# A retention block with an FP4 feed-forward on one core: z formed with tokens in rows, gate and up in three banks, set-up cut into five parts, a new order on every engine

## What is computed

```
Q = xpos(xn W_Q); K = xpos(xn W_K, downscale); V = xn W_V          # 8 heads of 32
scores = (Q K^T) * D,  D[n, m] = gamma_h^(n - m) for n >= m, else 0
Y = scores V;  Yn = (Y - mean) / sqrt(var + 1e-5) per head, times gn_weight, plus gn_bias
gate = silu(xn W_G);  retention = (gate * Yn) W_O
fp4(x): per block of 16 along the row, scale = max|x| / 6, x / scale rounded to the E2M1 grid, times scale
ffn = fp4(silu(fp4(xn) fp4(w_gate)^T) * (fp4(xn) fp4(w_up)^T)) fp4(w_down)^T       # inner width 704
```

## Time and profile before

| | us |
|---|---|
| median of 3 runs | 949.18 (949.08 to 950.0) |
| the profiled execution | 948.74 |
| its span | 946.9 |
| PE busy | 888.8 |
| DVE busy | 895.9 |
| ACT busy | 528.5 |
| POOL busy | 443.7 |

### The profile page before, as it was taken

The page is one execution under the profiler, slowest core; times in us unless marked ns, Lnnn a source line. Parts: engine busy times, 40 slices in busy tenths (PEclk is TensorE's granted clock), DMA queues, the critical chain, the costliest instruction groups (busy, mean ns, idle before and its releaser), DMA issues.

```text
span 946.9 us, 21085 instructions
## 1 busy us (share of the span) xinstructions
PE 888.8 (94%) x8258; PEld 798.1 (84%) x8258; DVE 895.9 (95%) x2220; ACT 528.5 (56%) x1331; POOL 443.7 (47%) x343
## 2 busy tenths in 40 slices
PE   0169999999999999999999999999999999999997
PEld 0158988898989899889988998998899889989986
DVE  5899999999999999999999999999999999999995
ACT  1345565556556655665555566556655655565553
POOL 3564544553454445444544444554445344444543
PEclk9999999999999999999999999999999999999999
DMA  9000000000000000000000000000000000000000
GB/s 281 40 1 12 24 12 24 23 24 13 24 23 19 18 24 24 12 24 24 24 12 24 24 19 17 23 24 12 24 23 24 14 24 23 18 19 24 12 7 17
DMA packets 28259, 24.95 MB, mean 26 GB/s; under 512 B 9088, under 2 KB 27648, under 8 KB 27904
## 3 DMA queue, kind: packets, MB, share of 16 engines
q1 hardware_dynamic: 20224, 18.95, 6.5%
q10 hardware_dynamic: 7936, 4.66, 1.7%
HBM read 15.21 MB, written 8.39 MB: 25 GB/s over the span
## 4 chain that ended last, share of the span: by engine, by line
PE 91%; DVE 5%; POOL 2%; ACT 1%; DMA 0%; issue 0%; SPq 0%; DVEq 0%; POOLq 0%
PE quad L775 11%; PE quad L773 11%; PE quad L774 11%; PE quad L844 4%; PE quad L908 4%; PE bank L850 3%; PE bank L855 3%; PE quad L901 3%; PE bank L774 3%; PE bank L775 3%; PE bank L773 3%; PE bank L830 3%; PE bank L862 3%; PE quad L869 3%; PE quad L878 2%; PE quad L877 2%
## 5 line engine op out<-in xcount | busy, mean ns | idle before, releaser
L392 POOL TENSOR_TENSOR h_quot<-h,h_inv 128x704 f32<-128x704 f32 x64 | 88.9, 1389 | 266.2 <-DVE h_inv L607 266.2
L388 POOL TENSOR_TENSOR rstd<-var_eps,power 128x9 f32<-128x9 f32 x67 | 158.0, 2358 | 38.6 <-DVE var_eps L557 38.5
L774 PE MATMUL quad<-w_gu_lo,xT_hi 128*128 128x352 f32 x512 | 165.1, 322 | 0.0
L775 PE MATMUL quad<-w_gu_hi,xT_lo 128*128 128x352 f32 x512 | 165.1, 322 | 0.0
L773 PE MATMUL quad<-w_gu_hi,xT_hi 128*128 128x352 f32 x512 | 165.0, 322 | 0.0
L376 POOL TENSOR_TENSOR zT_lo<-zT,zT_hi 128x256 fp32r<-128x256 f32 x64 | 51.8, 809 | 164.6 <-ACT zT_hi L677 164.6
L775 PEld LDWEIGHTS quad<-w_gu_hi,xT_lo 128*128 128x128 f32 x512 | 96.2, 188 | 0.0
L773 PEld LDWEIGHTS quad<-w_gu_hi,xT_hi 128*128 128x128 f32 x512 | 96.2, 188 | 0.0
L774 PEld LDWEIGHTS quad<-w_gu_lo,xT_hi 128*128 128x128 f32 x512 | 96.1, 188 | 0.0
L384 POOL TENSOR_TENSOR qk<-qk_cos,qk_sin 128x512 f32<-128x512 f32 x64 | 82.9, 1295 | 7.1 <-DVE qk_sin L531 6.5
L689 ACT ACTIVATE silu<-quad 128x352 f32<-128x352 f32 x64 | 29.8, 465 | 92.2 <-PE quad L775 92.2
(11 more groups left out here) (147 smaller groups left out, 2849.5 us busy)
## 6 DMA issues: line engine op xcount, KB each, us to landing
x_in<-in_L_attn_X_dram SPq DMA_DIRECT2D x64, 128.0 KB, 2.1
out_dram<-y_out SPq DMA_DIRECT2D x64, 128.0 KB, 1.7
sin<-const_sin_dram ACTq DMA_DIRECT2D x1, 2048.0 KB, 11.1
cos<-const_cos_dram ACTq DMA_DIRECT2D x1, 1024.0 KB, 6.4
raw<-in_L_ffn_w_down_dram SPq DMA_DIRECT2D x2, 352.0 KB, 4.0
raw<-in_L_ffn_w_gate_dram SPq DMA_DIRECT2D x1, 512.0 KB, 3.9
raw<-in_L_ffn_w_up_dram SPq DMA_DIRECT2D x1, 384.0 KB, 5.4
w_qkvg<-in_L_attn_W_Q_dram ACTq DMA_DIRECT2D x2, 128.0 KB, 5.0
```

The costliest lines, as they stand in the source:

```text
L388: pool.tensor_tensor(rstd[:], var_eps[:], power[:], ALU.pow).then_inc(rstd_ready, 1)
L392: pool.tensor_tensor(blocks(h_quot[:]), blocks(h[:]), spread(h_inv[:]), ALU.mult).then_inc(h_divided, 1)
L774: pe.matmul(out, hi[:, k], w_lo[:, k], start=False, stop=False)
L775: return pe.matmul(out, lo[:, k], w_hi[:, k], start=False, stop=stop)
```

## The change

The arithmetic of the result stays; what moves is where and when it is done.

1. **z with tokens in rows.** POOL multiplies the gate by weight and by bias, both broadcast over the partitions (`gate_gn`, 128x512), and by `rstd` (`y_gain`). DVE multiplies the transposed-back y by it (`y_part`, in place of `y_hat`), POOL adds the bias part (`z`). PE transposes z (two transposes in place of four), ACT copies the high part out of PSUM and DVE subtracts for the low part (in place of `zT` there and `zT_lo` on POOL). The two ACT instructions with weight and bias go.
2. **Gate and up in three banks.** The 1408 columns are reordered as 384 (the last 192 of gate and of up), 512 and 512. PE issues 6 matmuls of 384 and 12 of 512 columns for 24 of 352. Two of the three groups of tile i + 1 are done at the end of step i.
3. **Small work leaves DVE.** `x_shift`, `x_scale`, `h_scale` and `var_eps` go to POOL, the doubled 64 columns of `hq` to ACT. The reciprocal is taken of the maximum itself, and a factor of nearly 6 follows.
4. **Set-up.** The parts are cut as 768, 1024, 1024, 704 and 704 columns, each handled inside a step of the prologue or of step 0 and 1 (the parts 3 and 4, `w_down`). Three of five divisions move from POOL to DVE. The low part of a transposed weight comes from PE, which adds minus the high part to the transpose in PSUM, and ACT copies it. Loads are reissued in another order, x is loaded 7 tiles ahead by two semaphores, and only the first chunk of the tables is loaded early.
5. **Order.** All engines have a new order inside the step; the down projection of a tile moves wholly to the step two later.

The diff, cut to its core:

```diff
 G = 2
 HG = H // G
 F = 704
-FH = F // 2
+GW = 256
 CHUNKS = S // P
 TILES = B * CHUNKS
...
         b_xT = bank[0]
-        b_qk = b_qkT = bank[1]
-        b_gate = [bank[2], bank[4]]
-        b_up = [bank[3], bank[5]]
-        b_hT = [bank[1], bank[2]]
+        b_qk = bank[1]
+        b_qkT = bank[1]
+        b_gu = [bank[2], bank[3], bank[4][:, 0:2 * F - 4 * GW]]
+        b_vg = bank[5]
         b_kv = bank[3]
-        b_out = bank[4][:, 0:D]
-        b_vg = bank[6]
-        b_yT = [bank[5][:, 0:P], bank[6][:, 0:P]]
-        b_y = b_zT = bank[7]
-
-
+        b_yT = [bank[4][:, 0:P], bank[5][:, 0:P]]
+        b_y = bank[7][:, 0:D]
+        b_zT = bank[7][:, D:2 * D]
+        b_hT = [bank[0], bank[1]]
+        b_out = bank[6][:, 0:D]
+
+
...
+            sp.dma_start(raw_gu[:, 2, :], w_up[F - P:F, :]).then_inc(w_landed[0], 16)
+            sp.dma_start(raw_gu[:, 3:5, :], tiles_of(w_gate, 0, GW)).then_inc(w_landed[1], 16)
...
+                if exists(i + 2):
+                    t = i + 2
+                    pool.wait_ge(rstd_ready, t + 1)
+                    pool.tensor_scalar(x_shift[:], moments[:, 0:1], rstd[:, 0:1], -1.0, ALU.mult, ALU.mult).then_inc(x_shifted, 1)
+                if exists(i - 1):
+                    t = i - 1
+                    pool.wait_ge(rstd_ready, t + 4)
+                    pool.tensor_tensor(heads(y_gain[:]), heads(gate_gn[:, t % 2, 0, :]), spread(rstd[:, 1:], HD), ALU.mult).then_inc(gain_ready, 1)
+                if exists(i):
+                    t = i
+                    pool.wait_ge(rope_cos, t + 1)
+                    pool.tensor_tensor(qk[:], qk_cos[:], qk_sin[:], ALU.add).then_inc(rope_add, 1)
+                    if i == 0:
+                        size(3)
+                        divide(3)
+                    if i == 1:
+                        size(4)
+                        divide(4)
+                        out_low_parts()
+                if exists(i - 1):
+                    t = i - 1
+                    pool.wait_ge(y_scaled, t + 1)
+                    pool.tensor_tensor(z[:], y_part[:], gate_gn[:, t % 2, 1, :], ALU.add).then_inc(z_ready, 1)
+                if exists(i):
+                    t = i
+                    if t == 0:
+                        pool.wait_ge(gn_landed, 32)
+                    pool.wait_ge(gate_silu, t + 1)
+                    pool.tensor_tensor(gate_gn[:, t % 2, :, :], gate[:].unsqueeze(1).broadcast_to([P, 2, D]), gn[:], ALU.mult).then_inc(gate_scaled, 1)
+                    pool.wait_ge(h_inverted, t + 1)
+                    pool.tensor_tensor(blocks(h_quot[:]), blocks(h[:]), spread(h_inv[:]), ALU.mult).then_inc(h_divided, 1)
+                if exists(i + 2):
...
+                if exists(i + 2):
+                    t = i + 2
+                    pool.tensor_scalar(x_scale[:], x_max[:], 1.0 / 6.0, 1e-12, ALU.mult, ALU.max).then_inc(x_scaled, 1)
+                    if i == -2:
+                        qkvg_low_parts(0)
+                if exists(i) or exists(i + 3):
...
+                    if exists(t + 3):
+                        pool.wait_ge(x_moments, t + 4)
+                    pool.tensor_scalar(var_eps[:], moments[:, 1:], EPS, None, ALU.add).then_inc(var_ready, 1)
                     pool.wait_ge(var_ready, t + 4)
...
+            def largest(n):
+                cols, at = bounds(n)
+                dve.wait_ge(w_landed[n], 16 * PART_LOADS[n])
+                dve.tensor_reduce(w_max[:, at], blocks(raw[:, cols]), AX_X, ALU.max,
+                                  apply_absolute_value=True).then_inc(w_scaled[n], 1)
+
+            def invert(n):
+                cols, at = bounds(n)
+                dve.wait_ge(w_scaled[n], 1)
+                dve.reciprocal(w_rec[:, at], w_max[:, at]).then_inc(w_scaled[n], 1)
+                dve.wait_ge(w_scaled[n], 2)
+                dve.tensor_scalar(w_inv[:, at], w_rec[:, at], SIX, 1e12, ALU.mult, ALU.min).then_inc(w_scaled[n], 1)
+
+            def divide(n):
+                cols, at = bounds(n)
+                dve.wait_ge(w_scaled[n], 3)
+                dve.tensor_tensor(blocks(raw[:, cols]), blocks(raw[:, cols]), spread(w_inv[:, at]), ALU.mult).then_inc(w_divided, 1)
+
...
+                    dve.wait_ge(gain_ready, t + 1)
+                    dve.tensor_tensor(y_part[:], b_y[:, 0:D], y_gain[:], ALU.mult).then_inc(y_scaled, 1)
...
+                    if i == -3:
+                        largest(0)
+                        invert(0)
+                        divide(0)
...
+                    if i == -2:
+                        largest(1)
+                        invert(1)
+                        divide(1)
...
+                        dve.wait_ge(mask_landed, 16)
+                    dve.tensor_tensor(probs[:, 0:2, :], quad[:, 0:2, 0:G * P], mask, ALU.mult).then_inc(masked0, 1)
+                    if i == 0:
+                        round_off(3)
+                    if i == 1:
+                        round_off(4)
...
+                    if i == -1:
+                        largest(2)
+                        invert(2)
+                        divide(2)
+                        round_off(1)
+                        centre_values()
...
                     t = i - 1
+                    dve.wait_ge(z_high, t + 1)
+                    dve.tensor_tensor(zT_lo[:], tiles(b_zT), zT_hi[:].bitcast(F32), ALU.subtract).then_inc(z_low, 1)
...
+                    act.wait_ge(h_quant, t + 1)
+                    act.activation(hq[:, F:], hq[:, F - FL:F], ACT.Copy).then_inc(h_twice, 1)
...
+            def high_part(*groups):
+                for m in groups:
+                    hi, lo, shaped = weight_group(m)
+                    act.wait_ge(w_turned, m + 1)
+                    act.activation(hi, shaped(bank[HIGH_BANK[m]]), ACT.Copy).then_inc(w_high, 1)
+
+            def low_part(*groups):
+                for m in groups:
+                    hi, lo, shaped = weight_group(m)
+                    act.wait_ge(w_rest, m + 1)
+                    act.activation(lo, shaped(bank[LOW_BANK[m]]), ACT.Copy).then_inc(w_low, 1)
...
+                act.dma_start(cos[:, 1:, :], cos_d[:, 1:, :]).then_inc(tables_landed[1], 16)
+                act.dma_start(sin[:, 1:, :], sin_d[:, 1:, :]).then_inc(tables_landed[1], 16)
...
+                        turn(4, 5)
+                        turn_rest(4, 5)
+                    if t == 0:
+                        pe.wait_ge(w_low, 6)
+                    if t >= 1:
+                        pe.wait_ge(kv_add, kept_upto(t - 1))
+                    for k in range(KD):
+                        ins = product(b_gu[1], xT_hi[:, KD:], xT_lo[:, KD:], w_gu_hi[:, :, GU_COLS[2]], w_gu_lo[:, :, GU_COLS[2]],
+                                      k, start=k == 0, stop=k == KD - 1)
+                    ins.then_inc(gu_b_ready, 1)
...
+                    for k in range(KD):
+                        ins = pe.transpose(b_zT[:, k * P:(k + 1) * P], z[:, k * P:(k + 1) * P], ident[:])
...
+                    if i == -1:
+                        turn(0, 1)
+                        turn_rest(0, 1)
...
+            def turn_rest(*groups):
+
+                for m in groups:
+                    n, k = divmod(m, 2)
+                    hi, lo, shaped = weight_group(m)
+                    pe.wait_ge(w_high, m + 1)
+                    if 2 <= m <= 4:
+                        pe.wait_ge(w_low, (m - 1, m)[m == 4])
+                    b = bank[LOW_BANK[m]]
+                    for j, src in enumerate(sources(m)):
+                        pe.matmul(b[:, j * P:(j + 1) * P], src, ident[:], start=j == 0, stop=False, is_transpose=True)
+                    pe.matmul(shaped(b), ident_neg[:], hi, start=False, stop=True).then_inc(w_rest, 1)
...
+GU_COLS = [slice(0, 2 * (F - 2 * GW)), slice(2 * (F - 2 * GW), 2 * (F - GW)), slice(2 * (F - GW), 2 * F)]
+GU_PARTS = len(GU_COLS)
+PARTS = ([slice(c.start // P * D, c.stop // P * D) for c in GU_COLS]
          + [slice(NW * D + r * F, NW * D + (r + 1) * F) for r in range(KD)])
-PART_LOADS = [1, 4, 1, 1, 1]
-PART_GROUPS = [2] * len(PARTS)
+PART_LOADS = [4, 2, 2, 1, 1]
+HIGH_BANK = [6, 7, 6, 7, 6, 7, 6, 6, 6, 6]
+LOW_BANK = [1, 5, 1, 5, 5, 3, 6, 6, 6, 6]
```

1001 lines of the change are left out of this document (504 added, 497 removed).

## The result

| | before | after |
|---|---|---|
| median | 949.59 us (949.08 to 950.36, 4 runs) | 933.46 us (932.18 to 934.08, 4 runs) |
| the profiled execution, its span | 948.74, 946.9 | 933.82, 931.9 |

A forecast was written before the change was run, and what follows sets the result against it. PE was taken to pace the kernel, DVE 0.4 us a step behind; 948.7 less 15.9 (steady steps), 13.5 (set-up) and 3 (end) gave 916.3 us, predicted as 916; forecast 906 to 925, range 898 to 936.

The forecast's parts named there:

- The view of what bounds the kernel: Steady part: PE sets the pace at 13.70 us a step, with DVE 0.4 us behind it.
- The steady step: PE's step falls by 0.26 to 13.44 us, 15.9 us over 61 steps; DVE 12.4 us busy, POOL 9.2.
- DVE's stall in `x_diff`: Steady step on DVE: `x_diff`, slow beside POOL's addition for qk, drops from 799 to about 422 ns, saving 0.38 us.
- The rule on the shared port: DVE instructions with two SBUF inputs contend with POOL's SBUF reads; forecast trusted it for streaming work, not for `rstd`'s power.
- The rival in which the port makes the kernel slower: POOL's new streaming collides with DVE: steps up to 15.5 us, 1042 us in all; chance 0.07, shared with another ring.
- The set-up: Work ahead of tile 2: PE starts tile 2 near 70 us instead of 83.4, gaining 13.5 us (4 to 18).
- DVE's entry at 36: Before step 0: 26 us of DVE work, 5 of data waiting, about 2 for the first `xn`, 3 of collisions.
- The 15 and 17.5 us of steps 0 and 1: Lengths of steps 0 and 1: DVE's own work, some 10 and 12 us, plus parts 3 and 4 with collisions.
- DVE's own 4.3 plus 1 of collision each: Steps 0 and 1: DVE's work on parts 3 and 4 adds 4.3 us plus 1 of collision to each.
- the set-up gains nothing: Rival: set-up parts meet collisions and PE's serial turns in steps 0 and 1, 930 us; chance 0.22 shared with DVE bound.
- DVE takes over: Rival: DVE holds the step at 13.70, only set-up and end pay, 932 us; chance 0.22 shared with set-up without gain.
- The end: From tile 63's qk to the finish: about 24.5 us against 27.8, 3 us gained, between 0 and 6.

The follow-up runs named there:

- the three runs on the step: Changed kernel transposing z twice: 945.72 us; changed kernel with one more 256-column DVE instruction per step: 932.10; kernel before without gate's two transposes: 937.60.
- e6: Changed kernel with both loads moved, POOL's z, PE's turns and ACT's magnitude reordered, plus idle transposes in waits of steps 0 and 1: 927.26 us; without those transposes 927.08.

## Why the prediction was right in sign and half as large

**The view of what bounds the kernel: right.** PE paced before and paces after, shown by the three runs on the step.

**The steady step: right, somewhat small.** 13.44 was forecast, 13.43 is measured over the same 61 steps. That agrees by two errors which cancel: a step from tile 3 on is 13.393, and step 2, counted among the 61, is 2.2 us longer than the others (15.59). The 384-column interval was 0.17 us as interpolated. DVE's stall in `x_diff` went as said. DVE is busy 12.7 us a step (378.07 / 400 x 13.43), forecast 12.4, and POOL 9.26, forecast 9.2. There the single terms were off and made up for each other: `x_shift` took 669 and `h_scale` 387 ns, where 200 stood, and `rstd` fell from 2358 to 1835. Behind `x_shift` and `rstd` stand waits for DVE, told below.

**The rule on the shared port: against it for the power, with it for streaming work.** In the steady part `hq` takes 885 ns (880 before), though it starts beside the power, and the new streaming work of POOL cost DVE nothing that PE would feel. In the set-up the collision is real, and as long as the rule of the Trainium skill has it ("SBUF — State Buffer", section "Who interferes with whom"): POOL's low part of qkvg runs as two instructions, from 37.74 to 39.01 and from 38.97 to 40.44 us, and `x_diff` (37.99, 1.29 us) and `x_grid` (39.32, 1.40 us) each end about 0.3 us behind one of them, where 0.43 is their mean; the 5.41 us of the earlier trace rows ended 1.1 behind POOL's 4.73, and takes 1.22 alone. It also works the other way, which the prediction did not ask. In the kernel before, the power starts inside `h_grid` (512.64, 0.88 us) in every steady step and takes 2.38 us; in the changed kernel it starts ahead of it and takes 1.83:

```profile
512.80 2.38 POOL L388 TENSOR_TENSOR rstd<-var_eps,power 128x9 f32<-128x9 f32 x1 [0.45 <-DVE var_eps L557]
```

```profile
515.20 1.83 POOL L457 TENSOR_TENSOR rstd<-var_eps,power 128x9 f32<-128x9 f32 x1
```

```profile
515.51 0.89 DVE L678 SCALAR_TENSOR_TENSOR h_grid<-h_magic,h_diff 128x704 f16<-128x704 bf16 x1
```

The one power of the changed kernel that takes longer (2.41 us at 62.34) starts inside `hq`. In each of these cases 0.71 or 0.72 us of DVE's instruction are left when the power starts, so the 0.5 us that `rstd` fell by read as a wait for DVE. No run varies this by itself. The rival in which the port makes the kernel slower did not come.

**The set-up: this step failed.** "36 + 15 + 17.5 = 68.5, and PE starts tile 2 about 1.5 later, at 70." It was 85.58. With step 2, tile 3 came 17.7 us after the time that the forecast implies (70 + 13.44), which is the whole miss: 17.7, less 2.8 for the steady steps (60 x 0.047), plus 2.7 for the end, is 17.6, and the span is 17.4 us longer than forecast (931.9 against 914.5). Up to tile 2 the 15.6 us are 8.6 at DVE's entry, 7.8 in step 0 and 2.9 in step 1, less 3.7, since PE starts tile 2 2.2 us ahead of DVE's `qk_sin` of it (85.58, 87.75; 83.42, 85.61 before), not 1.5 behind: an error of the sum that worked in its favour. Its terms:
- DVE's entry at 36 was 44.63. The sum took 5 us of waiting for data, before the first tile. It didn't follow SP's queue, in which the load of tile 2 moved behind 0.5 MB of V and G, nor ask what ACT's tables do to it. That wait is 5.92 us, and moving the loads brings the entry to 39.3: shown, 5 to 6 us. DVE's work was right: 29.6 us busy up to there, where 29 stood (26 and 3 of collisions). Its idle time was not: 14.2 us in four waits (3.31 and 2.36 for the first data, 5.92, 2.62), where 7 stood. The 2.62 us for `x_magic` are a hand-over again: ACT has it behind the high copies of part 1, the first of which waits 3.81 us for PE's turn (35.26), and that turn had waited 2.10 us for DVE's rounding (34.11). No experiment removes that one.
- The 15 and 17.5 us of steps 0 and 1, which were 22.8 and 20.4. "The low parts on PE and the copies on ACT run beside DVE, PE being nearly idle then": cost nothing, it said. They cost 7.6 us for parts 3 and 4, and about 3.6 more for part 2. Being idle isn't the same as having slack: PE was idle because it waited for DVE's rounding, and each turn, copy, second turn and second copy then stood ahead of the products of the next tile.
- The low clock, 3 us, inside those steps. It was not in the sum. PE had stood idle in pieces ahead of it (0.71, 1.77 and 1.26 us, the last up to the turn at 59.26), and thirty transposes in those three waits kept the level up.
- DVE's own 4.3 plus 1 of collision each, 10.6 in all, was measured as 8.7: slightly too dear, but right. The base of 10 and 12 us was under the rows of before (11.2 and 13.3) and should have been those.

The rival "the set-up gains nothing" put 13.5 us back for this reason, PE's serial turns, and said 930; it is the one whose mechanism came. That "DVE takes over", 932, lies nearer the 933.46 is luck: its step of 13.70 was not there. The measured time lies inside the stated range of 898 to 936, outside the forecast's 906 to 925.

**The end: wrong, small.** 27.2 us from tile 63's qk, for 24.5 forecast and 27.8 before. The last row of DVE's timeline beside the earlier trace rows:

```profile
929.37 0.43 DVE L647 TENSOR_TENSOR y_out<-quad,x_in 128x256 f32<-128x256 f32 x1 [2.00 <-PE quad L979]
```

From DVE's last `qk_sin` it is 23.03 us, as it was 23.14: the chain as a whole is as long with tokens in rows. PE waits 3.02 us for POOL's `z` in it (920.58), and then works at the lower level, its 256-column products 0.21 us apart up to 924.3 where 0.12 is the steady interval; before, the like stretch was 939.3 to 942.6. No experiment took it apart.

**What stays open:** what the 2.1 us are by which step 0 is longer beyond all the turns, what holds step 1 when its waits are moved, what makes the end as long as before, and what the 0.07 us per steady step beyond the shapes are.

## What to carry to other kernels

Cost a prologue that is moved under the first steps as a chain across engines, not as busy time on the busiest one: an engine that idles there is mostly waiting, and each hand-over added to it lands ahead of the next tile's work. Follow each queue of DMA issues as an engine of its own, to the load that moved back in it. Where PE idles in pieces, look at the granted clock of the stretch, and at the intervals of its products, before costing what follows.

## What the runs showed that was not expected

- Thirty transposes whose result nobody reads made the kernel 3.0 us faster: the granted clock in 50 to 70 us was 1.00 with them, 0.91 and 0.74 without. In an order in which the clock stood at 1.00 there already, the same transposes gave nothing (e6).
- How long a short POOL instruction takes depends on what DVE runs beside it. `x_shift`, one column, takes 0.27 us alone (84.21 us) and 0.71 in the steady part, where it starts while DVE's `hq` runs (517.13, `hq` from 516.57 to 517.45), more than `y_gain` of 256 columns (0.61). `h_scale` on 44 columns takes 0.37 and `x_scale` on 16 takes 0.27, but 0.88 and 0.76 in steps 0 and 1, beside DVE's rounding of parts 3 and 4. The power on 9 columns is 1.83 us, or 2.38 when it starts inside such a DVE instruction.
- One DMA issue on SP took 2.99 us of the queue (`W_G`, 256 KB), that of a tile of x, 128 KB, 0.47.
